# Moving the load of a block's down weights to another queue, and its row numbers one block ahead

## The chip, the core and the metric

The kernel runs on one core of a Trainium2 chip. A core has TensorE (matrix products into PSUM), VectorE, ScalarE and GpSimd for elementwise work, and SyncE, which only issues DMAs. Each engine takes its own instructions in order; they meet by semaphores. DMAs can be issued from the queues of SyncE, ScalarE and GpSimd. The metric is the device time of one execution, in microseconds (us); a value given for a version is the median over runs.

## The reference

One decoder layer on 8 x 128 tokens of width 256: self-attention with a sliding window, cross-attention, and a mixture of 16 experts, top 4, with one shared expert. The part that matters here:

```python
routing_weights = jax.nn.softmax(x @ gate_w.T)             # 1024 tokens, 16 experts
topk_w, topk_ids = jax.lax.top_k(routing_weights, 4)
for e in range(16):
    coef = jnp.sum(jnp.where(topk_ids == e, topk_w, 0.0), axis=-1)
    h = silu_and_mul(x @ w13[e].T)                         # 256 -> 2 x 176 -> 176
    acc = acc + (h @ w2[e].T) * coef[:, None]              # 176 -> 256
out = silu_and_mul(x @ shared_gate_up_w.T) @ shared_down_w.T * sigmoid(x @ sgate_w.T) + acc
```

Everything is float32 with a loose tolerance only for rounding, so the kernel splits most operands of products into a high and a low part and adds three products (helper `three`, L1517).

## The kernel before

It has three stages. Up to about 160 us the attention layers run, tile after tile, with the routing of finished tiles in between. While the first half of the shared expert runs (`rows_of`, `down`), GpSimd scatters each token's normed row to four places in a DRAM table `x_slots` (L538), sorted by expert, and VectorE makes a table of blocks: an expert's rows are padded to whole blocks of 128, and there are always NBLK = 47 blocks. `table` holds for each block its expert and its first row. Then comes the stage of the blocks, and last the second half of the shared expert, the gathering of each token's four results, and the output.

The stage of the blocks is a software pipeline over n = 0 to 46, written out by hand on every engine. For block n:

- SyncE, `load_rows(n)` (L420): reads the first row's number from `table` into a register (L425) and loads 128 rows of 1072 bytes from `x_slots` into `xb` (L426). `xb` has RB = 4 buffers; from block 4 on it waits until TensorE has turned the buffer's previous block (`xbt_psum`) and VectorE has taken its row numbers (`ids_ready`).
- SyncE, `load_down(n)` (L428): reads the expert's number (L432) and loads its down weights, 256 KB, into `w2`, also with 4 buffers (L433); from block 4 on it waits for the down product of the buffer's previous block (`yb_psum`). Three `load_down` are issued as soon as the table is there; then SyncE waits for the scatters and issues `load_rows` 0 to 4, and then per step one `load_rows(n + 5)` and one `load_down(n + 3)`.
- TensorE: `turn_block(n)` (L1772) transposes `xb`; `block_up(n)` (L1524 by way of `three`) multiplies by gate and up weights, which all lie in SBUF; `turn_hidden(n)` (L1792) transposes the hidden rows; `block_down(n)` (L1802) multiplies by `w2`. In iteration n it does `turn_block(n + 2)`, `block_up(n + 1)`, `turn_hidden(n)`, `block_down(n - 1)`. Every fifth iteration it reads a word with six packed expert numbers between `block_up` and `turn_hidden` (L1751).
- ScalarE, in iteration n: `take_rows_t(n + 2)` (L812, the high part `xbt_h`), `block_gate(n + 1)` (L820, `sg`), `take_hidden_t(n)` (L827, `hbt`). Ahead of the loop it does the shared expert's last `high_hidden` (L749, `hid_h`), then `take_rows_t(0)`, `take_rows_t(1)` and `block_gate(0)`.
- VectorE, in iteration n: `low_rows_t(n + 2)` (L1270, `xbt_l`), `block_hidden(n + 1)` (L1278, `hb`), `block_ids(n + 1)` (L1290, L1293, L1294: which output row each row of the block goes to, and its coefficient), `take_block(n - 1)` (L1285, `yb`).
- GpSimd, `place_rows(n)` (L613): scatters `yb` to `y_picks` in DRAM by the numbers `ids`.

Of the kernel before, what the change touches and what calls it, by code (L numbers as in the profile page):

```python
# [17 lines left out]
B, T, D = 8, 128, 256  # L18
# [10 lines left out]
NE, HE, HS = 16, 176, 704  # L29
# [29 lines left out]
def decoder_layer(nc, x_in, ctx_in, keys_in, wqkv_in, bqkv_in, wo_in, bo_in, rope_in, masks_in, gate_in,  # L59
                  w13_in, w2_in, shared_in, ident_in, iota_in, tri_in, upto_in, table_in, picks_in, dump_in, packs_in, out):  # L60
    ctx = ExitStack()
    with ctx:
# [315 lines left out]
        @block.sync  # L378
        def _(sp):
            sp.dma_start(x[:, 0:2, 0:D], x_in[0:2].rearrange("b p d -> p b d")).then_inc(x_first, 16)  # L380
            sp.dma_start(wqkv[:, :, :], wqkv_in.rearrange("(k p) n -> p k n", p=128)).then_inc(wqkv_loaded, 16)
            sp.dma_start(rope[:, :, :], rope_in).then_inc(rope_loaded, 16)
            sp.dma_start(x[:, 2:B, 0:D], x_in[2:B].rearrange("b p d -> p b d")).then_inc(x_rest, 16)
            sp.dma_start(ctx_sb[:, :, :], ctx_in.rearrange("b p d -> p b d")).then_inc(ctx_loaded, 16)
            sp.dma_start(gate[:, :, :], gate_in.rearrange("(k p) n -> p k n", p=128)).then_inc(gate_loaded, 16)
            sp.dma_start(iota[:, :], iota_in.partition_broadcast(128)).then_inc(gate_loaded, 16)
            sp.dma_start(tri[:, :, :].bitcast(U16), tri_in).then_inc(gate_loaded, 16)
            sp.dma_start(upto[:, :], upto_in).then_inc(gate_loaded, 16)
            sp.dma_start(x[:, 0:B, D + TOPK:D + 2 * TOPK], picks_in).then_inc(gate_loaded, 16)
            sp.dma_start(dump[:, :], dump_in).then_inc(gate_loaded, 16)  # L390
            sp.dma_start(sw_raw[:, :], shared_in[0]).then_inc(sw_loaded, 16)

            def load_keys(c):

                if c:
                    sp.wait_ge(scores_psum[CROSS], 4 * c)
                sp.dma_start(ktc[:, :, :, :].rearrange("p u v n -> p (u v n)"), keys_in[c]).then_inc(ktc_loaded, 16)

            load_keys(0)
            for i in range(4):  # L400
                es = slice(4 * i, 4 * i + 4)
                sp.dma_start(w13[:, es, :, :], w13_in[:, es, :, :]).then_inc(w13_loaded, 16)
            sp.wait_ge(zeros_ready, 1)
            for c in range(1, B):
                load_keys(c)
                if 2 <= c <= SC:
                    sp.wait_ge(swl_ready, c - 1)
                    sp.dma_start(sw_raw[:, :], shared_in[c - 1]).then_inc(sw_loaded, 16)
                if c == 1:
                    sp.dma_start(x_slots[EMPTY:EMPTY + 128, :], zero_b[:, :].bitcast(F32)).then_inc(rows_zeroed, 16)  # L410
                for e in range(NZERO * (c - 1), min(NZERO * c, NE)):
                    sp.dma_start(x_slots[REGION * e:REGION * e + REGION, :].rearrange("(p r) d -> p r d", p=128),
                                 zero_b[:, :].bitcast(F32).unsqueeze(1).broadcast_to([128, REGION // 128, XW])
                                 ).then_inc(rows_zeroed, 16)

            sp.wait_ge(swl_ready, SC)
            sp.dma_start(ends[:, :, :, :], table_in).then_inc(table_loaded, 16)
            sp.dma_start(packs[:, :], packs_in).then_inc(table_loaded, 16)

            def load_rows(n):  # L420

                if n >= RB:
                    sp.wait_ge(xbt_psum, n - RB + 1)
                    sp.wait_ge(ids_ready, n - RB + 1)
                row = sp.value_load(table[0:1, NBLK + n:NBLK + n + 1], min_val=0, max_val=EMPTY)  # L425
                sp.dma_start(xb[:, n % RB, :], x_slots[bass.ds(row, 128), :]).then_inc(xb_loaded[n % RB], 16)  # L426

            def load_down(n):  # L428

                if n >= RB:  # L430
                    sp.wait_ge(yb_psum, n - RB + 1)
                e = sp.value_load(table[0:1, n:n + 1], min_val=0, max_val=NE - 1)  # L432
                sp.dma_start(w2[:, n % RB, :, :].rearrange("p k d -> p (k d)"),  # L433
                             w2_in[bass.ds(e, 1)].rearrange("e p k d -> p (e k d)")).then_inc(w2_loaded[n % RB], 16)

            sp.wait_ge(x3_ready, B)
            sp.wait_ge(table_ready, 3)
            for n in range(RB - 1):
                load_down(n)
            sp.wait_ge(scattered, 16 * TOPK * B)  # L440
            for n in range(RB + 1):
                load_rows(n)
            for n in range(NBLK):
                if n + RB + 1 < NBLK:
                    load_rows(n + RB + 1)
                if n + RB - 1 < NBLK:
                    load_down(n + RB - 1)
            for r in range(RB):
                sp.wait_ge(yb_placed[r], 16 * len(range(r, NBLK, RB)))
            for b in range(B):  # L450
                sp.dma_start(yg[:, b, :, :], y_picks[T * TOPK * b:T * TOPK * (b + 1), :].rearrange("(p k) d -> p k d", k=TOPK)
                             ).then_inc(gathered[b], 16)

            for pair in range(HB // 2):
                sp.wait_ge(x_out_ready, pair + 1)
                sp.dma_start(out[2 * pair:2 * pair + 2].rearrange("b p d -> p b d"), x2[:, 2 * pair:2 * pair + 2, :]
                             ).then_inc(y_stored, 16)
            for b in range(HB, B):
                sp.wait_ge(x_out_ready, HB // 2 + b - HB + 1)
                sp.dma_start(out[b], x2[:, b, :]).then_inc(y_stored, 16)  # L460
            sp.wait_ge(y_stored, 16 * (HB // 2 + HB))
# [159 lines left out]
        def _(act):  # L621
# [185 lines left out]
            def take_rows_t(n):  # L807

                act.wait_ge(xbt_psum, n + 1)
                if n >= 2:  # L810
                    act.wait_ge(gu_psum, n - 1)
                act.activation(xbt_h[:, n % 2, :, :], ps_xt[n % 2][:, 0:KC * 128].rearrange("p (k n) -> p k n", k=KC),  # L812
                               ACT.Copy).then_inc(xbt_high, 1)
# [8 lines left out]
            def take_hidden_t(n):  # L822

                act.wait_ge(hbt_psum, n + 1)
                if n >= 2:
                    act.wait_ge(yb_psum, n - 1)
                act.activation(hbt[:, n % 2, :, :], ps_ht[n % 2][:, 0:KC * 128].rearrange("p (k n) -> p k n", k=KC),  # L827
                               ACT.Copy).then_inc(hbt_ready, 1)

            take_rows_t(0)  # L830
            take_rows_t(1)
            block_gate(0)
            for n in range(NBLK):
                if n + 2 < NBLK:
                    take_rows_t(n + 2)
                if n + 1 < NBLK:
                    block_gate(n + 1)
                take_hidden_t(n)
# [8 lines left out]
        def _(dve):  # L847
# [419 lines left out]
            def low_rows_t(n):  # L1267

                dve.wait_ge(xbt_high, n + 1)
                dve.tensor_tensor(xbt_l[:, n % 2, :, :], ps_xt[n % 2][:, 0:KC * 128].rearrange("p (k n) -> p k n", k=KC),  # L1270
                                  xbt_h[:, n % 2, :, :].bitcast(F32), ALU.subtract).then_inc(xbt_low, 1)

            def block_hidden(n):

                dve.wait_ge(sg_ready, n + 1)
                if n >= 2:
                    dve.wait_ge(hbt_psum, n - 1)
                dve.tensor_tensor(hb[:, n % 2, 0:HE], sg[:, n % 2, :], ps_gu[n % 2][:, HE:GU], ALU.mult).then_inc(hb_ready, 1)  # L1278
# [8 lines left out]
            def block_ids(n):  # L1287

                dve.wait_ge(xb_loaded[n % RB], 16 * (n // RB + 1))
                link(dve.scalar_tensor_tensor(found[:, n % 2, :, :], xb[:, n % RB, D:D + TOPK].unsqueeze(1).broadcast_to([128, 2, TOPK]),  # L1290
                                              of_block[:, n:n + 1], xb[:, n % RB, D + TOPK:XW].rearrange("p (i k) -> p i k", i=2),
                                              ALU.is_equal, ALU.mult))
                link(dve.tensor_reduce(offset[:, n % RB, :], found[:, n % 2, :, :], AX.X, ALU.add))  # L1293
                dve.scalar_tensor_tensor(ids[:, n:n + 1], offset[:, n % RB, 0:1], UNPLACED, dump[:, n:n + 1], ALU.add, ALU.min  # L1294
                                         ).then_inc(ids_ready, 1)

            dve.wait_ge(table_ready, 3)
            low_rows_t(0)
            low_rows_t(1)
            block_hidden(0)  # L1300
            block_ids(0)
            for n in range(NBLK):
                if n + 2 < NBLK:
                    low_rows_t(n + 2)
                if n + 1 < NBLK:
                    block_hidden(n + 1)
                if n + 1 < NBLK:
                    block_ids(n + 1)
                if n >= 1:
                    take_block(n - 1)  # L1310
            take_block(NBLK - 1)
# [607 lines left out]
```

## Time and profile before

| What | Value |
|---|---|
| time, median of 3 runs | 344.32 us (343.75 to 344.35) |
| the profiled execution | 343.41 us, of which the span is 341.6 us |
| busy, share of the span: PE / PEld / DVE / ACT / POOL | 90% / 70% / 71% / 55% / 43% |
| mean rate of the DMAs over the span | 196 GB/s |
| DMA queue of SyncE (q1), share of 16 engines | 55.0% |
| DMA queue of ScalarE (q10), share of 16 engines | 1.2% |
| down weights: issues, size, median time to landing | 47, 256.0 KB, 3.1 us |
| rows of a block: issues, size | 47, 134.0 KB |

PE is TensorE's products, PEld its weight loads, which overlap with them; DVE is VectorE, ACT ScalarE, POOL GpSimd. A "q" behind an engine's name marks its queue: register work, waits and the issue of DMAs, which aren't counted as busy. In a timeline the figure in brackets is how long the engine stood idle before the instruction and what ended that. The granted clock is TensorE's, as a share of 2.4 GHz.

### The profile page before, as it was taken

The numbers are of one execution on the slowest core, as the hardware profiler recorded it, in microseconds if no ns is written. First come the engines' busy times: TensorE is split into PE (matmuls) and PEld (weight loads), VectorE is DVE, ScalarE is ACT, GpSimd is POOL, SyncE is SP. The second block draws the span as 40 slices with busy tenths as digits, with TensorE's granted clock in tenths as the row PEclk, the third lists the DMA queues.
The fourth block names the chain that finished last, engine by engine and source line by source line (L and its number), as shares of the span: only waits on it lengthen the run. The fifth ranks groups of instructions, "written<-read, shape, count | busy, mean of one in ns | idle before, by whom it ended". The sixth has DMA issues, their size and how long they took to land.

```text
span 341.6 us, 8504 instructions
## 1 busy us (share of the span) xinstructions
PE 308.8 (90%) x2606; PEld 238.2 (70%) x2608; DVE 241.5 (71%) x720; ACT 186.7 (55%) x538; POOL 146.6 (43%) x179
## 2 busy tenths in 40 slices
PE   6897899999999997879997789998999989999983
PEld 2354576667667764658775578787978979888862
DVE  2357788988888799563887856576766666765396
ACT  1052889888898977473697333343434434342231
POOL 3584133544544413487578253333434434345000
PEclk9999999999999998996999989999999999999998
DMA  7997197989899941023122526777777777774681
GB/s 210 302 389 307 25 310 179 302 248 291 242 264 266 239 141 33 16 98 113 54 94 96 157 66 187 214 218 233 209 230 210 220 224 213 229 220 149 249 319 61
DMA packets 44153, 66.84 MB, mean 196 GB/s; under 512 B 5347, under 2 KB 31988, under 8 KB 43604
## 3 DMA queue, kind: packets, MB, share of 16 engines
q1 hardware_dynamic: 39476, 54.91, 55.0%
q0 software_dynamic: 3792, 10.56, 8.1%
q10 hardware_dynamic: 848, 0.92, 1.2%
q8 instruction: 19, 0.31, 0.4%
q14 instruction: 18, 0.15, 0.2%
HBM read 37.07 MB, written 29.30 MB: 194 GB/s over the span
## 4 chain that ended last, share of the span: by engine, by line
PE 53%; DVE 9%; DMA 8%; issue 8%; SPq 8%; POOL 7%; ACT 6%; DVEq 0%; ACTq 0%; POOLq 0%
PE bank L1524 16%; PE bank L1802 6%; DMA xb<-x_slots 6%; POOL x_slots L538 5%; PE bank L1441 5%; PE bank L1450 5%; ACT probs L650 4%; PE bank L1394 3%; PE bank L1459 3%; SPq L425 3%; PE bank L1772 2%; SPq L432 2%; PE bank L1483 2%; PE bank L1792 2%; PE bank L1562 2%
## 5 line engine op out<-in xcount | busy, mean ns | idle before, releaser
L613 POOL DMA_INDIRECT y_picks<-yb,ids x47 | 45.1, 960 | 70.0 <-DVE yb L1285 69.4
L650 ACT ACTIVATE probs<-bank,neg_max 128x128 f32<-128x128 f32 x256 | 70.7, 399 | 2.7 <-DVE neg_max L903 2.5
L1802 PE MATMUL bank<-w,hbt 128*128 128x256 f32 x188 | 48.3, 380 | 0.0
L903 DVE TENSOR_REDUCE neg_max<-bank 128x4 f32<-128x512 f32 x64 | 42.1, 683 | 5.8 <-PE bank L1441 5.7
L1450 PE MATMUL bank<-ident,probs 128*128 128x128 f32 x256 | 36.9, 281 | 2.6 <-ACT probs L650 2.6
L812 ACT ACTIVATE xbt_h<-bank 128x256 fp32r<-128x256 f32 x47 | 18.0, 384 | 38.5 <-PE bank L1772 38.4
L538 POOL DMA_INDIRECT x_slots<-x,slots x32 | 34.5, 1080 | 9.3 <-issue 8.9
L1450 PEld LDWEIGHTS bank<-ident,probs 128*128 128x128 f32 x256 | 29.1, 143 | 12.4 <-ACT probs L650 10.3
L1802 PEld LDWEIGHTS bank<-w,hbt 128*128 128x128 f32 x188 | 32.1, 190 | 2.5
L1278 DVE TENSOR_TENSOR hb<-sg,bank 128x176 f32<-128x176 f32 x47 | 15.9, 337 | 24.0 <-ACT sg L820 24.0
L820 ACT ACTIVATE sg<-bank 128x176 f32<-128x176 f32 x47 | 14.9, 317 | 30.2 <-PE bank L1524 30.2
L1270 DVE TENSOR_TENSOR xbt_l<-bank,xbt_h 128x256 fp32r<-128x256 f32 x47 | 19.9, 424 | 11.6 <-ACT xbt_h L812 8.6
L1524 PE MATMUL bank<-w_h,xbt_h 128*128 x94 | 27.5, 373 | 0.0
L1772 PE MATMUL bank<-ident,xb 128*128 128x128 f32 x94 | 18.9, 284 | 6.8 <-DMA xb<-x_slots 6.5
L1285 DVE TENSOR_SCALAR yb<-bank,offset 128x256 f32<-128x256 f32 x47 | 22.7, 483 | 2.0 <-PE bank L1802 2.0
L1524 PE MATMUL bank<-w_h,xbt_l 128*128 x94 | 23.4, 331 | 0.0
L1524 PE MATMUL bank<-w_l,xbt_h 128*128 x94 | 23.3, 330 | 0.0
L1772 PEld LDWEIGHTS bank<-ident,xb 128*128 128x128 f32 x94 | 12.0, 143 | 15.2 <-DMA xb<-x_slots 9.2
L509 POOL TENSOR_TENSOR rstd<-ve,expo 128x1 f32<-128x1 f32 x16 | 9.1, 570 | 26.0 <-DVE ve L953 26.0
L485 POOL TENSOR_TENSOR turned<-qkv,rope 128x320 f32<-128x320 f32 x8 | 6.9, 863 | 29.5 <-DVE qkv L884 29.5
L827 ACT ACTIVATE hbt<-bank 128x256 f32<-128x256 f32 x47 | 18.0, 383 | 1.8 <-PE bank L1792 1.8
L1792 PE MATMUL bank<-ident,hb 128*128 128x128 f32 x94 | 18.0, 273 | 0.7 <-issue 0.5
(175 smaller groups left out, 677.6 us busy)
## 6 DMA issues: line engine op xcount, KB each, us to landing
x_slots<-zero_b SPq DMA_DIRECT2D x16, 1072.0 KB, 10.9
w<-w_in_dram SPq DMA_DIRECT2D x47, 256.0 KB, 3.1
xb<-x_slots SPq DMA_DIRECT2D x47, 134.0 KB
w<-w_in_dram SPq DMA_DIRECT2D x4, 1408.0 KB, 12.6
yg<-y_picks SPq DMA_DIRECT2D x8, 512.0 KB, 7.0
sw_raw<-shared_in_dram SPq DMA_DIRECT2D x6, 384.0 KB, 3.4
ktc<-keys_in_dram SPq DMA_DIRECT2D x8, 256.0 KB, 3.2
ctx_sb<-ctx_in_dram SPq DMA_DIRECT2D x1, 1024.0 KB, 12.6
```

Source lines behind the costliest of these rows:

```text
L538: pool.indirect_dma_start(x_slots[:, :], bass.IndirectOffsetOnAxis(slots[:, TOPK * b + k:TOPK * b + k + 1], 0), x[:, b, :], None).then_inc ...
L613: pool.indirect_dma_start(y_picks[:, :], bass.IndirectOffsetOnAxis(ids[:, n:n + 1], 0), yb[:, n % RB, :], None).then_inc(yb_placed[n % RB] ...
L650: ins = act.activation(probs[:, g, j, :], ps_s[kind][g][:, 128 * j:128 * j + 128], ACT.Exp, bias=neg_max[:, kind, g, j:j + 1])
L812: act.activation(xbt_h[:, n % 2, :, :], ps_xt[n % 2][:, 0:KC * 128].rearrange("p (k n) -> p k n", k=KC), ACT.Copy).then_inc(xbt_high, 1)
L903: dve.tensor_reduce(neg_max[:, kind, g, :], ps_s[kind][g].rearrange("p (j n) -> p j n", j=BLK), AX.X, ALU.max, negate=True).then_inc(max_r ...
L1270: dve.tensor_tensor(xbt_l[:, n % 2, :, :], ps_xt[n % 2][:, 0:KC * 128].rearrange("p (k n) -> p k n", k=KC), xbt_h[:, n % 2, :, :].bitcast( ...
L1285: dve.tensor_scalar(yb[:, n % RB, :], ps_yb[n % 2][:, 0:D], offset[:, n % RB, 1:2], None, ALU.mult).then_inc(yb_ready, 1)
L1450: ins = pe.transpose(ps_s[kind][g][:, 128 * j:128 * j + 128], probs[:, g, j, :], ident[:, :])
L1524: ins = pe.matmul(outs, w, m, start=first and i == 0, stop=last and i == len(todo) - 1, skip_group_check=not (first and last))
L1772: ins = pe.transpose(ps_xt[n % 2][:, 128 * k:128 * k + 128], xb[:, n % RB, 128 * k:128 * k + 128], ident[:, :])
L1792: ins = pe.transpose(ps_ht[n % 2][:, 128 * k:128 * k + 128], hb[:, n % 2, 128 * k:128 * k + 128], ident[:, :])
L1802: ins = pe.matmul(ps_yb[n % 2][:, 0:D], hbt[:, n % 2, k, :], w2[:, n % RB, k, :], start=k == 0, stop=k == KC - 1)
```

## The change

The 47 `load_down` move from SyncE's instructions to ScalarE's. Ahead of ScalarE's loop four of them are issued, for blocks 0 to 3, behind two waits for the table and the attention; in its iteration n, from 2 on, `load_down(n + 2)` stands between `take_rows_t(n + 2)` and `block_gate(n + 1)`. SyncE keeps `load_rows` in its old order. On VectorE `block_ids(0)` and `block_ids(1)` stand ahead of `block_hidden(0)`, and iteration n has `block_ids(n + 2)` in place of `block_ids(n + 1)`.

```diff
--- before.py
+++ after.py
@@ -425,26 +425,14 @@
                 row = sp.value_load(table[0:1, NBLK + n:NBLK + n + 1], min_val=0, max_val=EMPTY)
                 sp.dma_start(xb[:, n % RB, :], x_slots[bass.ds(row, 128), :]).then_inc(xb_loaded[n % RB], 16)
 
-            def load_down(n):
-
-                if n >= RB:
-                    sp.wait_ge(yb_psum, n - RB + 1)
-                e = sp.value_load(table[0:1, n:n + 1], min_val=0, max_val=NE - 1)
-                sp.dma_start(w2[:, n % RB, :, :].rearrange("p k d -> p (k d)"),
-                             w2_in[bass.ds(e, 1)].rearrange("e p k d -> p (e k d)")).then_inc(w2_loaded[n % RB], 16)
-
             sp.wait_ge(x3_ready, B)
             sp.wait_ge(table_ready, 3)
-            for n in range(RB - 1):
-                load_down(n)
             sp.wait_ge(scattered, 16 * TOPK * B)
             for n in range(RB + 1):
                 load_rows(n)
             for n in range(NBLK):
                 if n + RB + 1 < NBLK:
                     load_rows(n + RB + 1)
-                if n + RB - 1 < NBLK:
-                    load_down(n + RB - 1)
             for r in range(RB):
                 sp.wait_ge(yb_placed[r], 16 * len(range(r, NBLK, RB)))
             for b in range(B):
@@ -827,12 +815,26 @@
                 act.activation(hbt[:, n % 2, :, :], ps_ht[n % 2][:, 0:KC * 128].rearrange("p (k n) -> p k n", k=KC),
                                ACT.Copy).then_inc(hbt_ready, 1)
 
+            def load_down(n):
+
+                if n >= RB:
+                    act.wait_ge(yb_psum, n - RB + 1)
+                e = act.value_load(table[0:1, n:n + 1], min_val=0, max_val=NE - 1)
+                act.dma_start(w2[:, n % RB, :, :].rearrange("p k d -> p (k d)"),
+                              w2_in[bass.ds(e, 1)].rearrange("e p k d -> p (e k d)")).then_inc(w2_loaded[n % RB], 16)
+
+            act.wait_ge(x3_ready, B)
+            act.wait_ge(table_ready, 3)
+            for n in range(RB):
+                load_down(n)
             take_rows_t(0)
             take_rows_t(1)
             block_gate(0)
             for n in range(NBLK):
                 if n + 2 < NBLK:
                     take_rows_t(n + 2)
+                if n >= 2 and n + RB - 2 < NBLK:
+                    load_down(n + RB - 2)
                 if n + 1 < NBLK:
                     block_gate(n + 1)
                 take_hidden_t(n)
@@ -1297,15 +1299,16 @@
             dve.wait_ge(table_ready, 3)
             low_rows_t(0)
             low_rows_t(1)
+            block_ids(0)
+            block_ids(1)
             block_hidden(0)
-            block_ids(0)
             for n in range(NBLK):
                 if n + 2 < NBLK:
                     low_rows_t(n + 2)
                 if n + 1 < NBLK:
                     block_hidden(n + 1)
-                if n + 1 < NBLK:
-                    block_ids(n + 1)
+                if n + 2 < NBLK:
+                    block_ids(n + 2)
                 if n >= 1:
                     take_block(n - 1)
             take_block(NBLK - 1)
```

## Rows read from the trace of the kernel before

**Rows 1.** groups, 204 to 314 us: busy us, mean ns, idle us, releaser

```profile
L1792 PEld LDWEIGHTS bank<-ident,hb 128*128 128x128 f32 x90 | 12.4, 141 | 2.6 <-issue 1.7
L1772 PEld LDWEIGHTS bank<-ident,xb 128*128 128x128 f32 x86 | 10.9, 141 | 10.9 <-DMA xb<-x_slots 7.8
```

**Rows 2.** timeline of ScalarE: start us, duration us, operation, idle before

```profile
203.03 0.38 ACT L812 ACTIVATE xbt_h<-bank 128x256 fp32r<-128x256 f32 x1
...
205.25 0.38 ACT L812 ACTIVATE xbt_h<-bank 128x256 fp32r<-128x256 f32 x1 [0.70 <-PE bank L1772]
...
207.51 0.38 ACT L812 ACTIVATE xbt_h<-bank 128x256 fp32r<-128x256 f32 x1 [0.70 <-PE bank L1772]
...
307.94 0.38 ACT L812 ACTIVATE xbt_h<-bank 128x256 fp32r<-128x256 f32 x1 [0.70 <-PE bank L1772]
```

**Rows 3.** timeline of SyncE's queue: start, duration of its DMA issues

```profile
213.06 0.34 SPq L433 DMA_DIRECT2D w<-w_in_dram  x1
214.24 0.34 SPq L426 DMA_DIRECT2D xb<-x_slots  x1
215.44 0.34 SPq L433 DMA_DIRECT2D w<-w_in_dram  x1
...
217.72 0.75 SPq L433 DMA_DIRECT2D w<-w_in_dram  x1
```

**Rows 4.** single lines, durations in ns: number reads and a ScalarE DMA

```profile
L425 SPq TENSOR_LOAD <-table x47: 262/268/503, 193.9 to 303.4; - x47
...
L1751 PEldq TENSOR_LOAD <-words x8: 299/308/572, 191.4 to 273.8; - x8
...
L623 ACTq DMA_DIRECT2D bqkv<-bqkv_in_dram x1: 450/450/450, 1.2 to 1.2; - x1
```

**Rows 5.** chain of the work that ended last, 204 to 312 us: start, duration

```profile
231.13 4.30 DMA xb<-x_slots
```

**Rows 6.** TensorE's word read near 225, a product behind it, a weight load

```profile
L1751 PEldq TENSOR_LOAD <-words x1: 301/301/301, 225.0 to 225.0; - x1
...
225.16 0.56 PE L1524 MATMUL bank<-w_h,xbt_h 128*128 x2
...
251.42 0.20 PEld L1792 LDWEIGHTS bank<-ident,hb 128*128 128x128 f32 x2 [0.53 <-issue]
```

**Rows 7.** timeline of all engines, one block's step

```profile
204.83 0.38 PE L1772 MATMUL bank<-ident,xb 128*128 128x128 f32 x2
...
206.21 0.32 ACT L820 ACTIVATE sg<-bank 128x176 f32<-128x176 f32 x1 [0.58 <-PE bank L1524]
...
206.43 0.38 ACT L827 ACTIVATE hbt<-bank 128x256 f32<-128x256 f32 x1
206.56 0.34 DVE L1278 TENSOR_TENSOR hb<-sg,bank 128x176 f32<-128x176 f32 x1 [0.47 <-ACT sg L820]
...
207.26 0.16 DVE L1294 SCALAR_TENSOR_TENSOR ids<-offset,dump 128x1 uint32<-128x1 f32 x1
...
208.28 0.38 PE L1792 MATMUL bank<-ident,hb 128*128 128x128 f32 x2
```

**Rows 8.** timeline of all engines, start of the block stage

```profile
194.87 0.63 ACT L749 ACTIVATE hid_h<-hid 128x512 fp32r<-128x512 f32 x1 [2.38 <-DVE hid L1174]
...
197.19 0.38 ACT L812 ACTIVATE xbt_h<-bank 128x256 fp32r<-128x256 f32 x1 [1.69 <-PE bank L1772]
197.68 0.42 DVE L1270 TENSOR_TENSOR xbt_l<-bank,xbt_h 128x256 fp32r<-128x256 f32 x1 [0.67 <-ACT xbt_h L812]
...
198.49 0.68 PE L1524 MATMUL bank<-w_h,xbt_h 128*128 x2
```

**Rows 9.** busy time by stretch: length, engines (count), granted clock, DMA share, GB/s

```profile
195.00:196.00 1.00, 0.00 (x0) 0.00 (x0) 1.00 (x3) 0.50 (x1) 0.00 (x0) 1.00 0.39 106
199.00:200.00 1.00, 1.00 (x5) 1.00 (x4) 0.42 (x1) 0.15 (x1) 1.00 (x2) 0.50 0.56 129
264.00:276.00 12.00, 11.89 (x73) 10.54 (x72) 8.23 (x31) 5.03 (x15) 4.79 (x5) 1.00 0.78 225
```

## The prediction

> **What bounds the kernel now.** I first asked for the groups of instructions in the stage of the expert blocks (204 to 314 us, nearly a third of the span) and read the column of idle time. TensorE's weight loads stood 7.8 us there for a block's rows, `xb`, to land, and 1.7 us more on nothing that the profile shows [rows 1]. No row shows a wait for `w2`. Then the time of one block: ScalarE takes the turned rows once a block (`xbt_h`). From the take at 203.03 to the one at 307.94 there are 43 steps, 104.91 us, a mean of 2.44; 28 of the 43 last at most 2.33, and the pair in between that is shown is 2.26 apart [rows 2]. I take 2.27 as the step in which TensorE waits for nothing: 43 x 2.27 = 97.6, so 7.3 us are lost in this stage, and that is all that a change of the queues can win in it.
>
> Why are rows late? SyncE issues two loads a block, and its timeline shows a new DMA every 1.18 to 1.20 us, alternately weights and rows [rows 3]. Two loads are 2.38, more than 2.27, without any wait. SyncE's queue, always running, is slower than TensorE; it falls behind until a row load is issued so late that its 4.30 us to land show [rows 5]. A load is mostly not the DMA: reading the number from SBUF takes 0.27, the DMA 0.34, the rest is register work [rows 3, 4].
>
> Four of the long steps have another cause: TensorE's own read of a packed word stood between two products (steps of 2.70, 2.75, 2.68 and 2.56, together 1.6 us over the pace; the row is such a stop, of 0.53) [rows 6]. The other 5.7 us are `xb`.
>
> **The change, part by part.**
>
> *SyncE loses a load per block.* It keeps about 1.20 us of work per step of 2.27. Its queue stops being late: gain up to 5.7 us. The word read also gains some. At 225.0 it ran before the products ahead of it in the program began (225.16), and that step was not long; it stops TensorE where the queue had just been held up [rows 6]. With rows always early, between none and all of the 1.6 us goes; I take half, 0.8. Sum of the gain: 6.5 us, bounds 5.7 and 7.3.
>
> *Row numbers one block further ahead.* The three small VectorE operations of a block (the last one in the row at 207.26) are the same in number. They free `xb` for SyncE. In the block that is shown, rows were turned at 204.83, and VectorE's numbers in that iteration ended at 207.42 [rows 7]. After the change those are the numbers of the block just turned; before, of the one ahead of it. So a buffer is free 2.6 us after its turn, or 3.05 with the 0.45 us that I put on ScalarE below; 0.85 for the register work brings the DMA to 3.9, and the longest landing of 4.30 to 8.2, against four steps, 9.08, until the buffer's next block is due [rows 5, 7]. With the numbers a step later it would be 10.5, so without this part the wait on the numbers would replace SyncE's slowness in the worst landings. At the start two blocks' numbers, not one, come ahead of the first `hb`: 0.6 us more on VectorE (hidden rows are multiplied at 206.56 for 0.34, numbers end at 207.42), beside the first up product, which takes longer. I cost it at nothing; uncovered it would be 0.6 once.
>
> *ScalarE gains a load per block.* No row shows a number read into a register on ScalarE. Nearest from below: SyncE's whole load, 1.20 [rows 3]. From above: TensorE's read is 0.31 instead of 0.27 and ScalarE's own DMA issue at the kernel's start 0.45 instead of 0.34, which makes 1.20 + 0.04 + 0.11 = 1.35 [rows 4]. A gain is excluded, since nothing is taken off ScalarE. I take 1.24, the row nearest in kind for the read and SyncE's DMA for the same transfer. It is queued behind `xbt_h` and ahead of `sg` and `hbt`; its added wait is for a down product that precedes the turn for which `xbt_h` waits, so it is always met. In the shown block `xbt_h` starts at 205.25, so a load that starts with it ends near 206.55 to 206.65, and `sg` goes from 206.21 to about 206.65, `hbt` from 206.43 to 206.87, `hb` from 206.56 to 207.0, ending 207.35 [rows 2, 7]. TensorE needs that `hb` at 208.28. There are 0.9 us of cover, ScalarE is through by 207.25 and its next turn comes at 207.51. Cost on the path: nothing. This stands on the load running beside `xbt_h` (0.38) and not after it, as the word read at 225.0 ran beside TensorE's products. If the cover is gone, each 0.1 us per block is 4.3 us.
>
> *Four loads before the first block, on ScalarE.* Before, SyncE asked for three of them long before. Now they stand in ScalarE's queue behind the `hid_h` of 194.87 and ahead of the first `xbt_h`, which ran at 197.19 [rows 8]. Starting at 194.9, 4 x 1.24 = 4.96, so `xbt_h` at 199.9 instead of 197.19. From its start to the end of the first `xbt_l` it was 0.91 (197.19 to 198.10); the first up product so starts near 200.8 instead of 198.49: loss 2.3 us. Lower bound nothing, if ScalarE's queue can read ahead while `hid_h` waits; upper bound 4 x 1.35 (2.7) and 0.7 for the clock, 3.4. The clock: TensorE did nothing in the us after 195, and the granted clock was 0.50 in the us after 199, so 1.2 of 2.4 GHz [rows 9]. A longer stand has the same low stretch coming, not a second one, so I put nothing for it; 0.7 is one more up product at that level. The next thing late there is nothing: all four rows have landed by then, and `w2` is needed one block later.
>
> At one place a rule speaks against the change. In the stretch 264 to 276 the 16 DMA engines were busy 0.78 of the time at 225 GB/s [rows 9]; all of it is needed at any pace, and at 2.27 instead of the mean of 2.36 of the five steps that lie in that stretch it would be 0.81. The Trainium skill (DMA: Bandwidth & Descriptors, Issuing engines are not separate DMA queues) says that DMAs from any engine share the same 16 DMA engines, and that issuing from several saves only issue time. If transfers were the limit, the sum by that rule would be the loss at the start alone, 346.6, which is the second rival; the rows have issue time as the limit (two loads of 1.19 against 2.27), and where that holds the rule allows the gain.
>
> **The sum.** The profiled execution took 343.41, 341.6 of it the span. Minus 6.5, plus 2.3: 339.2. What follows the blocks starts from their end and moves with it. The median of the three runs is 0.9 above the profiled one, so I forecast 344.32 - 4.2 = 340.1 us, with its own range of 338.9 to 341.7 (gain 5.7 to 7.3, loss 1.9 to 3.1).
>
> **Rivals.**
> 1. *ScalarE becomes the bound (slower).* Place: the block loop. If the load doesn't run beside `xbt_h`, ScalarE's step is 0.38 + 1.24 to 1.35 + 0.32 + 0.38 = 2.32 to 2.43 [rows 2, 7]. From 2.37 on (2.27 + 4.2/43) nothing is won. At 2.43 it is 43 x 0.16 = 6.9 more, 347.0; one DMA issue of SyncE took 0.75 instead of 0.34 [rows 3], and if such collisions between two queues came in each block it would be far more. For: only 0.9 us of cover for a thing never seen on this engine. Against: the word read at 225.0 ran ahead of queued products, and ScalarE has 0.58 and 0.70 us idle in the shown step [rows 2, 7]. Beside it stands a sentence of the Trainium skill (Perfetto Trace Analysis, DMA Instruction — HWDGE): a sequencer locks the descriptor generator for itself, which could make two queues wait for each other; no run here shows it yet.
> 2. *The transfers are the limit.* If rows land later now that weights come on another queue at the same time, half of the 5.7 stays: 340.1 + 2.9 = 343.0; all 6.5 stay, with the start's loss: 346.6. For: 0.81 busy and a landing of up to 4.30 [rows 5, 9]. Against: in the same stage 28 steps ran at the pace, and the lead is 9.08.
> 3. *The start costs nothing*, because ScalarE's queue reads ahead: 344.3 - 6.5 = 337.8. Against: TensorE's word read, too, came only after its queue's waits had been met.
> 4. *It doesn't do what it says*: SyncE would then still be late for the numbers. That is 344 to 346.6.
>
> **How the numbers follow.** Forecast 0.56, ScalarE the bound 0.17, transfers 0.13, the start free 0.11, the last 0.03. The range leaves out most of the first rival and the worst of the second, about 0.18: 337.7 to 345.0. A measurement of this kernel can tell about 0.2% from no change, 0.7 us. Faster: the forecast, the free start, half of the transfers' cases (0.06): 0.73. Slower: most of ScalarE's cases and the worst of the others, 0.18. Within 0.2%: the rest, 0.09.
>
> **What would show it.** In the profile after: TensorE's idle for `xb` in the block stage near zero (right: under 1 us; wrong: over 3); steps between two `xbt_h` at 2.27 throughout (ScalarE as bound: even steps of 2.32 or more, with no idle ahead of `xbt_h`); the first `xbt_h` near 199.9 and the first up product near 200.8; ScalarE's loads at 1.2 to 1.35; `sg` about 0.45 later behind `xbt_h`. The forecast is wrong if TensorE's weight loads wait for `hb` or `hbt`, or if rows still arrive late with SyncE idle.

## The result, and the profile after

The changed kernel took 340.41 us against 343.18 of the kernel before, medians of 20 runs each, taken side by side; the ratio is 0.989, with a 95% interval of 0.986 to 0.992. This ratio is of the fast runs alone (7 of the 20 after lie over 1.5% above that kernel's fastest run and are left out); the two medians, over all runs, give 0.992. The forecast was 340.1. The profiled execution took 339.23 (span 337.4) against 343.41 (span 341.6), 4.2 less.

Where the 4.2 us lie is read from three points: the start of the last `hid_h` ahead of the blocks, the `xbt_h` of block 3 and that of block 46. From `hid_h` to block 46 the profiled execution took 113.07 us before (194.87 to 307.94) [rows 2, 8] and 109.20 after, 3.9 less. What lies ahead of it ended 0.2 earlier, and what follows, 33.7 us, is 0.1 shorter. So in this pair the change acts in this stage alone, in two parts of opposite sign. (How long the work ahead takes varies: in a second profile of the same changed kernel, a0 below, `hid_h` starts at 198.16 instead of 194.68. That is why stages are compared here and not spans.)

The first is the loop. The groups of the block stage after, as in [rows 1]: busy us, mean ns, idle us and releaser.

```profile
L1795 PEld LDWEIGHTS bank<-ident,hb 128*128 128x128 f32 x94 | 13.4, 143 | 1.2 <-issue 0.2
L1775 PEld LDWEIGHTS bank<-ident,xb 128*128 128x128 f32 x88 | 12.4, 142 | 5.4 <-DMA xb<-x_slots 1.3
```

TensorE's wait for rows fell from 7.8 to 1.3 us, and the stop that no row explained, the word read's, from 1.7 to 0.2. The 43 steps took 98.53 (205.35 to 303.88) instead of 104.91; 40 of them last at most 2.33.

The second part is the start. Timeline of all engines after, as in [rows 8]; the figure in brackets is the idle time before an instruction:

```profile
194.68 0.63 ACT L737 ACTIVATE hid_h<-hid 128x512 fp32r<-128x512 f32 x1 [2.39 <-DVE hid L1176]
195.64 3.56 ACTq L823 DMA_DIRECT2D w<-w_in_dram  x4
199.24 0.66 ACT L800 ACTIVATE xbt_h<-bank 128x256 fp32r<-128x256 f32 x2 [3.93 <-issue]
...
200.30 0.95 PE L1527 MATMUL bank<-w_h,xbt_h 128*128 x2 [3.22 <-DVE xbt_l L1272]
```

ScalarE's four loads fill the time from 195.64 to 199.20. From `hid_h` to the first up product it is now 5.62 instead of 3.62 us (194.87 to 198.49), and to the `xbt_h` of block 3, 10.67 instead of 8.16. The missing half us is the clock: the first two up products took 0.95 instead of 0.68 (198.49 in [rows 8]), and the turn of the hidden rows 0.62 instead of 0.40, here after and then before:

```profile
204.41 0.62 PE L1795 MATMUL bank<-ident,hb 128*128 128x128 f32 x2
202.32 0.40 PE L1792 MATMUL bank<-ident,hb 128*128 128x128 f32 x2
```

Busy time by stretch, as in [rows 9] (the granted clock is the third figure from the end):

```profile
200.00:201.00 1.00, 0.70 (x2) 0.71 (x3) 1.00 (x3) 0.00 (x0) 1.00 (x1) 0.50 0.73 209
203.00:204.00 1.00, 1.00 (x5) 1.00 (x4) 0.57 (x2) 0.27 (x1) 0.00 (x0) 0.50 0.23 21
204.00:205.00 1.00, 1.00 (x7) 0.93 (x6) 0.00 (x1) 0.32 (x1) 0.00 (x0) 0.55 0.47 125
```

And two stretches of the kernel before:

```profile
202.00:203.00 1.00, 1.00 (x8) 0.93 (x8) 0.12 (x2) 0.47 (x2) 0.00 (x0) 0.83 0.00 0
203.00:204.00 1.00, 1.00 (x9) 0.98 (x8) 0.93 (x5) 0.47 (x3) 0.00 (x0) 1.00 0.46 117
```

After TensorE's longer stand (3.22 us idle ahead of the product at 200.30) the clock was still at 0.50 (1.2 GHz) in the us after 203; before, it was full by then. A stretch of 1 us at 0.83 or 0.55 is a mix of 0.50 and 1.00 (at 1.00 for 0.66 and for 0.10 of it), so the clock rose at 202.3 before and at 204.9 after. By the same reading of the us after 198 (0.97 before, 0.53 after) it fell at 198.9 and 198.1: it was low for 3.4 us before and for 6.8 after. The start so lost 2.5 us, the loop won 6.4, and 6.4 - 2.5 = 3.9.

One more thing is new. The queue of SyncE, 206 to 300 us (line, what it waited for, us in all, times, longest), and the issues of the two loads with their median time to landing, in us:

```profile
SPq L424 <- DVE ids L1296: 41.3, 40, 1.6
```

```profile
w<-w_in_dram ACTq DMA_DIRECT2D x47, 256.0 KB, 4.3
xb<-x_slots SPq DMA_DIRECT2D x47, 134.0 KB, 4.2
```

SyncE, which before waited 2.5 us for row numbers in four waits, now waits 1 us for those of each block. And weights take 4.3 us to land, from the issue of the DMA to the arrival of its data, which took 3.1.

### The profile page after: what moved, and what is told of

It reads as the page before. It is cut to its first block, busy times and chain, and to the rows that moved or that the text cites. A ratio compares the mean times of both kernels' runs of the same rounds, so it can differ in the third digit from the quotient of the medians.

```text
span 337.4 us, 8509 instructions
## 1 busy us (share of the span) xinstructions
PE 306.1 (91%) x2608; PEld 238.9 (71%) x2608; DVE 238.8 (71%) x720; ACT 186.4 (55%) x538; POOL 146.6 (43%) x179
## 4 chain that ended last, share of the span: by engine, by line
PE 65%; DVE 13%; ACT 10%; DMA 4%; issue 4%; ACTq 2%; POOL 1%; SPq 0%; DVEq 0%; POOLq 0%
PE bank L1527 22%; PE bank L1805 10%; PE bank L1444 5%; PE bank L1453 4%; ACT probs L638 4%; PE bank L1397 3%; DMA xb<-x_slots 3%; PE bank L1775 3%; PE bank L1795 3%; PE bank L1486 2%; PE bank L1462 2%; PE bank L1565 2%; PE bank L1501 2%; PE bank L1439 2%; DVE neg_max L905 1%
## 5 line engine op out<-in xcount | busy, mean ns | idle before, releaser
L1775 PEld LDWEIGHTS bank<-ident,xb 128*128 128x128 f32 x94 | 13.2, 144 | 8.2 <-issue 2.7
```

The lines of the kernel that those rows point to most:

```text
L1775: ins = pe.transpose(ps_xt[n % 2][:, 128 * k:128 * k + 128], xb[:, n % RB, 128 * k:128 * k + 128], ident[:, :])
```

## The experiments

The numbers of all of them together. Ratio: to the kernel before on the same chip, with its interval. Start: from `hid_h` to the first up product. Loop: the 43 steps from block 3 to block 46. Stage: from `hid_h` to the `xbt_h` of block 46. Landing: medians of rows and weights, over those of the 47 loads for which the profile gives a landing (a dash where it gives none; for rows it gives 23 after, 11 in e8 and 47 in e1 again). The last four columns are of the profiled execution, in us.

| kernel | time | ratio | start | loop | stage | landing |
|---|---|---|---|---|---|---|
| before | 343.18 | 1 | 3.62 | 104.91 | 113.07 | - / 3.1 |
| after | 340.41 | 0.989 [0.986, 0.992] | 5.62 | 98.53 | 109.20 | 4.2 / 4.3 |
| a0, after again | 340.75 | 0.991 [0.987, 0.995] | 5.62 | 97.74 | 108.57 | 4.2 / 4.3 |
| e2, queue alone | 351.67 | 1.022 [1.017, 1.028] | 5.62 | 112.18 | 122.74 | 3.7 / 3.6 |
| e3, numbers alone | 340.46 | 0.989 [0.983, 0.995] | 3.43 | 100.97 | 109.11 | 2.7 / 3.1 |
| e1, loads in a gap | 338.96 | 0.985 [0.980, 0.990] | 3.31 | 99.29 | 107.30 | 4.1 / 4.2 |
| e4, SyncE filled again | 343.93 | 1.000 [0.996, 1.005] | 5.62 | 102.63 | 113.30 | 3.8 / - |
| e5, half the weights | 339.48 | 0.989 [0.985, 0.992] | 2.62 | 101.40 | 108.52 | 2.4 / 2.5 |
| e6, one read more | 340.36 | 0.994 [0.991, 0.997] | 5.59 | 98.05 | 108.84 | 2.9 / 3.1 |
| e7, two reads more | 348.85 | 1.017 [1.010, 1.024] | 5.57 | 105.90 | 116.32 | 2.8 / 3.1 |
| e1 again | 338.07 | 0.984 [0.979, 0.988] | 3.39 | 98.24 | 106.24 | 4.3 / 4.4 |
| e8, gap and behind `hbt` | 336.83 | 0.981 [0.976, 0.986] | 2.62 | 96.62 | 105.34 | 3.1 / 3.2 |

The same kernel's stage differs by 0.6 us (after and a0) to 1.1 (e1 twice) from one profiled execution to another; less than that proves nothing.

**The whole change once more**, beside the first experiments.

> The changed kernel again, as the base of the other runs on this chip. In its profile the 43 steps from the take of block 3's rows to that of block 46's took 98.5 us instead of 104.9, and the take of block 3 stood 2.3 us later than before. Theory (late rows were SyncE's issue time, four loads now stand ahead of the first take): the same again, 4 us less than the kernel before, ratio 0.986 to 0.992. Rival (a chance of two traces): the steps come out at 101 us or more, ratio 0.995 or above.

The loop took 97.74 and the stage 108.57: again 7.2 won in the loop and 2.7 lost at the start.

**The queue alone.** The row numbers stay where they were before:

```diff
-            block_ids(0)
-            block_ids(1)
             block_hidden(0)
+            block_ids(0)
...
-                if n + 2 < NBLK:
-                    block_ids(n + 2)
+                if n + 1 < NBLK:
+                    block_ids(n + 1)
```

> The changed kernel without its second part: the down weights stay on ScalarE's queue, the row numbers come where they were before. Theory of the prediction (the numbers free the buffers, and a step later the landing no longer fits into four steps): numbers end 4.9 + 0.45 us after a block's turn, 0.85 for the read, and a landing of 4.2 make 10.4 against 9.08, so the step goes to 2.4 to 2.6, TensorE waits for xb in most steps, and the time is 3 to 12 us above the full change, no better than before. Rival (the queue alone was the cause, the numbers are an addition that does nothing): steps at 2.27 to 2.32, within 1 us of the full change.

2.2% slower than before. SyncE waited 51.2 us for numbers. The chain of the work that ended last, 291 to 300 us, names every link (start, duration):

```profile
286.32 5.54 DMA xb<-x_slots
...
291.91 0.45 PE bank L1774 x2
292.38 0.28 ACT xbt_h L800
...
293.06 0.34 ACTq L823
...
293.50 0.33 ACT sg L808
293.85 0.34 DVE hb L1280
294.19 0.15 DVE found L1292
294.36 0.17 DVE offset L1295
294.56 0.17 DVE ids L1296
...
294.80 0.27 SPq L425
...
295.52 3.76 DMA xb<-x_slots
299.28 0.04 issue
299.32 0.45 PE bank L1774 x2
```

It is a ring. The turn at 291.91 is that of block 36; the numbers at 294.56 are those of block 35, and free the buffer of block 39, which is turned at 299.32. The ring spans three steps, and its time is 3.61 to the issue (291.91 to 295.52) plus the landing. With the median landing of 3.7 a step is (3.6 + 3.7)/3 = 2.43, with the 5.54 of the landing before it in this chain 3.05; the mean step, 2.61, lies between them. With the numbers one step earlier the same ring spans four steps, and even with 5.5 it is (3.6 + 5.5)/4 = 2.28. That is what the second part of the change is worth: without it the first part makes the kernel slower.

**The numbers alone.** The reverse: SyncE keeps both loads, only VectorE's order is that of after.

```diff
-            block_hidden(0)
             block_ids(0)
+            block_ids(1)
+            block_hidden(0)
...
-                if n + 1 < NBLK:
-                    block_ids(n + 1)
+                if n + 2 < NBLK:
+                    block_ids(n + 2)
```

> The kernel before with only its row numbers one block further ahead. Theory (SyncE's queue is the limit by its own instructions, two loads of 1.19 us a block): steps stay at a mean of 2.40 to 2.45, 103 to 105 us for 43, time within 1 us of before. Rival (the wait for the numbers held SyncE up): steps fall to 99 to 101 us, time 3 to 5 us less, which would make the queue's move needless.

This edit of a few lines gives as much as the whole change. In the loop it won 3.9 us, at the start it lost nothing. SyncE waited for numbers no more, and its DMAs come as follows (timeline of its queue):

```profile
207.08 0.34 SPq L426 DMA_DIRECT2D xb<-x_slots  x1
208.19 0.34 SPq L433 DMA_DIRECT2D w<-w_in_dram  x1
209.35 0.34 SPq L426 DMA_DIRECT2D xb<-x_slots  x1
210.46 0.34 SPq L433 DMA_DIRECT2D w<-w_in_dram  x1
211.62 0.34 SPq L426 DMA_DIRECT2D xb<-x_slots  x1
```

Two loads are 1.11 + 1.16 = 2.27 us, exactly TensorE's step. There is no reserve, and single hold-ups of 0.1 to 0.9 us between two issues are never made up: from the row load at 209.35 to that at 301.84 there are 39 steps, a mean of 2.37. Groups, 204 to 314 us:

```profile
L1773 PEld LDWEIGHTS bank<-ident,xb 128*128 128x128 f32 x88 | 11.6, 141 | 8.0 <-DMA xb<-x_slots 4.5
```

TensorE still waits 4.5 us for rows, and the loop is 3.4 over 97.6. This is the part that moving the load can win.

**SyncE filled again.** The changed kernel, with two number reads, unused, behind every row load of SyncE:

```diff
                 sp.dma_start(xb[:, n % RB, :], x_slots[bass.ds(row, 128), :]).then_inc(xb_loaded[n % RB], 16)
+                for _ in range(2):
+                    sp.value_load(table[0:1, n:n + 1], min_val=0, max_val=NE - 1)
```

> The full change with two reads of a number that nobody uses behind each row load on SyncE, 0.57 us each, so that SyncE is again as busy as with two loads (1.13 + 1.14 = 2.27 us a block) while bytes, queues of the transfers and row numbers stay. Theory (SyncE as busy as TensorE's step of 2.27 has no reserve: each hold-up spends lead that never comes back): the 43 steps go from 98 to 101 to 104 us, time 2.5 to 5.5 us above the full change. Rival (what made rows late was the order of the transfers on one queue, not SyncE's instructions): steps at 98 to 99, time within 1 us of the full change.

No wait for numbers is left in SyncE's queue. Its row loads follow each other by 2.25 us at the least and 2.41 in the mean (206 to 300 us), and the loop is 102.63, 4.1 to 4.9 over the change. TensorE waits for rows:

```profile
L1777 PEld LDWEIGHTS bank<-ident,xb 128*128 128x128 f32 x88 | 11.6, 143 | 8.5 <-DMA xb<-x_slots 5.4
```

With weights on another queue and numbers early, SyncE's instructions alone bring the loss back. Its issue time does count.

**Half the weights.** The kernel before with the same instructions, but half the bytes of each weight load (the product uses the first half twice, so the second half of `w2` is left out):

```diff
-                sp.dma_start(w2[:, n % RB, :, :].rearrange("p k d -> p (k d)"), ...
+                sp.dma_start(w2[:, n % RB, 0, :], ...
...
-                    hbt[:, n % 2, k, :], w2[:, n % RB, k, :], ...
+                    hbt[:, n % 2, k, :], w2[:, n % RB, 0, :], ...
```

> The kernel before with half of each block's down weights left out of the load (the second half of the product uses the first half's weights), instructions on SyncE the same. Theory (SyncE's instructions): a row lands a little sooner behind a shorter transfer, 0.3 to 1.5 us once or twice over the whole loop; steps 103 to 104.5 us, time 0.3 to 1.5 us below before. Rival (the 16 DMA engines are the limit, or the landing is): steps at 98 to 100, time 4 us or more below before.

I was wrong here: 3.9 us faster, though SyncE issues as much as ever. Rows landed in 2.4 us, at most 3.2 (of the 12 for which the profile gives it), SyncE waited 0.2 us for numbers instead of 2.5, and the loop was 101.40. In the kernel before, then, bytes are not without a price. I put it down to the ring of [rows 5, 7] (2.59 us from a turn to the end of the next numbers, 207.42 - 204.83, and 0.85 of register work): it takes (3.44 + 4.30)/3 = 2.58 a step with the longest landing and (3.44 + 3.2)/3 = 2.21 with 3.2, so in the longest landings it had no more reserve than SyncE. (Of the 4.6 us that the stage won here 1.0 lie at the start, 3.5 in the loop.)

**Reads on ScalarE.** The changed kernel with one (e6) or two (e7) more unused number reads behind each `load_down` in ScalarE's loop; the edit for one:

```diff
                 if n >= 2 and n + RB - 2 < NBLK:
                     load_down(n + RB - 2)
+                    act.value_load(table[0:1, n:n + 1], min_val=0, max_val=NE - 1)
```

> The full change with one more read of a number per block on ScalarE, behind the load, about 0.66 us. Theory (ScalarE's load lies beside xbt_h and has about 1.0 us of cover ahead of the hb that TensorE needs, and ScalarE's queue is full at about 2.25 a block then): steps between 2.27 and 2.33, 0 to 3 us more. Rival (the load already lies on the path): the step grows by the whole read, 2.9, 27 us more.

> The full change with two more reads per block on ScalarE, 1.3 us. Theory: now ScalarE's queue is the bound, 1.24 for the load, 1.32 for the reads and some 0.35 for handing out three activations, 2.9 a step: 43 x 0.63, 27 us more, with TensorE waiting for hb or hbt. Rival (ScalarE's queue is not the limit even so, or each read counts fully from the first): 0 to 5 us, or 54 us more.

One read costs nothing in the loop (98.05): the cover that the prediction named is there. (The ratio is 0.994 against 0.989 for the change alone, with intervals that overlap.) Two are past its end. Waits of e7, 206 to 300 us:

```profile
ACT sg L808 <- issue: 52.0, 33, 1.8
...
PEld bank L1797 <- DVE hb L1282: 5.8, 16, 0.5
```

Now TensorE waits for `hb`, and steps last 2.46 in the mean, with no idle time ahead of `xbt_h`: the first rival, made real by two reads. Its step is smaller than I expected, so a read costs ScalarE less than I put.

**The loads in a gap.** ScalarE waits 2.4 us ahead of the last `hid_h`. Two loads are put there, behind `gate(SC + 1)`; the others follow in the loop, two blocks ahead instead of four:

```diff
             gate(SC + 1)
+            act.wait_ge(table_ready, 3)
+            for n in range(2):
+                load_down(n)
             high_hidden(SC + 1)
...
-            act.wait_ge(x3_ready, B)
-            act.wait_ge(table_ready, 3)
-            for n in range(RB):
-                load_down(n)
             take_rows_t(0)
...
-                if n >= 2 and n + RB - 2 < NBLK:
-                    load_down(n + RB - 2)
+                if n + 2 < NBLK:
+                    load_down(n + 2)
```

> The changed kernel with only the loads of blocks 0 and 1 ahead of the loop, and those in ScalarE's idle time ahead of the last hid_h (192.3 to 194.7 us in its profile); block n + 2 is loaded in every iteration n from 0. Theory (the start's loss is the four loads in ScalarE's queue): the first up product comes back to 198.3 to 198.9 from 200.3, the steps stay near 98.5, the time is 1.2 to 2.3 us less than with the change alone, 336.9 to 338.0 where that is 339.2. Rival (the first rows or the low granted clock set the start, not ScalarE): the first up product moves by less than 0.5 us and the time with it.

> The version with two weight loads in ScalarE's gap ahead of hid_h, once more, beside the next kernel. Both theories: 338 to 340 us, a ratio of 0.983 to 0.989; rows land 4.0 to 4.2 us after their issue in the median, weights 4.2; 43 steps of 98 to 99.3 us; first up product 3.3 us after the start of hid_h.

Timeline of ScalarE and TensorE in the first of the two:

```profile
194.01 1.46 ACTq L797 DMA_DIRECT2D w<-w_in_dram  x2
196.09 0.63 ACT L737 ACTIVATE hid_h<-hid 128x512 fp32r<-128x512 f32 x1 [2.38 <-DVE hid L1175]
197.56 0.38 ACT L811 ACTIVATE xbt_h<-bank 128x256 fp32r<-128x256 f32 x1 [0.84 <-PE bank L1774]
199.40 0.67 PE L1526 MATMUL bank<-w_h,xbt_h 128*128 x2
```

The wait ahead of `hid_h` is the 2.38 it was; the loads lie in it, and the first up product follows 3.31 us after `hid_h` again. (It stands at 199.40 and not at 198.3 to 198.9, since `hid_h` came 1.4 us later than in the profile after.) The loss at the start was the four loads in ScalarE's queue, and it was avoidable. The low stretch of the clock is back to 3.4 us as well: all six profiles with the four loads ahead of the loop show 6.8 us, the other six 3.4. (In time, e1 is 1.8 us below a0 on the same chip, with intervals that overlap.)

**The load behind `hbt`.** Row loads and weight loads of the changed kernel are issued almost together, and both land late. This kernel is that with the loads in the gap, with the loop's load moved:

```diff
-                if n + 2 < NBLK:
-                    load_down(n + 2)
                 if n + 1 < NBLK:
                     block_gate(n + 1)
                 take_hidden_t(n)
+                if n + 2 < NBLK:
+                    load_down(n + 2)
```

> As the version with the loads in the gap, but in the loop ScalarE's weight load stands behind hbt instead of behind xbt_h, so that it is issued about 1 us away from SyncE's row load. Theory A, rows and weights land late (4.1 and 4.2 instead of 2.7 and 3.1 us) because the two queues issue at the same moment: both medians fall to 3.0 to 3.4, 43 steps of 97.6 to 98.2, 0 to 1.5 us below the version in the gap. Theory B, they land late because of the bytes asked for at this pace, whenever they are issued: medians stay at 4.0 to 4.3, steps and time as in the version in the gap within 0.7 us. Theory C, the load now delays xbt_h (by 0.6 us): TensorE waits for xbt_h, 43 steps of over 100, slower than the version in the gap by 2 us or more.

The issues of a block, first in the changed kernel, then in this one (timeline of the two queues), and this one's issues with their landing:

```profile
227.35 0.37 ACTq L823 DMA_DIRECT2D w<-w_in_dram  x1
227.41 0.34 SPq L426 DMA_DIRECT2D xb<-x_slots  x1
```

```profile
226.06 0.34 ACTq L797 DMA_DIRECT2D w<-w_in_dram  x1
...
227.17 0.34 SPq L426 DMA_DIRECT2D xb<-x_slots  x1
```

```profile
w<-w_in_dram ACTq DMA_DIRECT2D x47, 256.0 KB, 3.2
xb<-x_slots SPq DMA_DIRECT2D x47, 134.0 KB, 3.1
```

Over the 35 row loads between 212 and 292 us, a row load follows the weight load ahead of it by a median of 0.33 us in the changed kernel, 0.24 in e1 again and 1.14 here. Against e1 again, rows land in 3.1 instead of 4.3 us and weights in 3.2 instead of 4.4, at no lower rate of bytes (235 GB/s from 206 to 300, against 232). In e6, where the extra read made it 0.88, they land in 2.9 and 3.1. So it is the moment of issue and not the amount.

Which neighbour matters is not shown, and one run speaks against the row load. In e4 a row load stands 1.30 us behind the weight load ahead of it and 0.97 ahead of the next (medians of the 33 in that stretch), and rows still land in 3.8. A third transfer of each block is GpSimd's scatter of results. By the starts that the profile gives, the weight load nearest to a scatter is a median of 0.14 us from it in the changed kernel, 0.22 in e1 again, 0.16 in e2 and 0.13 in e4, where rows land late, but 0.64 in e6, 0.86 in e3, 1.03 in e7 and 1.00 here, where they land early. So it may be the weights and the scatter that must be kept apart; no run moved the scatter alone.

The loop is the shortest of all, 96.62 (its first step is short, since the `xbt_h` of block 3 was 0.7 late), with no wait of TensorE for rows. At 336.83 this is by its median the fastest kernel of the study, 1.9% below the kernel before; its gain over e1 beside it on the same chip, 1.2 us, lies within the two intervals.

## Why the prediction was right, and where it wasn't

**The sum held.** Predicted: 6.5 won in the loop and 2.3 lost at the start. Measured: 6.4 and 2.5 in the first profile, 7.2 and 2.7 in the second. In time the fall is 2.8 us between the medians (3.7 by the ratio), where 4.2 was forecast. That 340.41 still lies 0.3 from 340.1 is in part luck: the kernel before took 343.18 beside it, and 344.32 in the three runs that the forecast started from. The signs came nearly as described: 1.3 us of waiting for rows (under 1 was asked, over 3 would have been wrong), the first `xbt_h` at 199.24 (199.9) and the first up product at 200.30 (200.8).

**Its account of the loop was half right.** The step "two loads are 2.38, more than 2.27" took its interval where a number read of SyncE was slow (0.36 us at 214.63, instead of 0.27, makes the 1.20 in [rows 3]); unheld, e3 shows 2.27. It is only with hold-ups that SyncE's mean is 2.37. And the prediction gave all of the 5.7 us of `xb` to this one cause. There were two rings without reserve: SyncE's instructions, and the buffer's way from turn to numbers to landing. In the loop 104.91 goes to 100.97 with the numbers alone, and from there to 97.7 to 98.5 with the weights on the other queue: 3.9 for the part that I costed at nothing, 2.4 to 3.2 for the part to which I gave everything. That split holds in this order only: taken first, the moved load costs 7.3 (e2), and the numbers then win 13.7 (112.18 to 98.53). Within the sum, the word read's stops fell by 1.5 (1.7 to 0.2), where 0.8 was taken.

**"The wait on the numbers would replace SyncE's slowness in the worst landings" was too mild.** The prediction had the number and didn't make it a price: 10.5 us for four steps is 2.62 a step and 112.9 for 43, and e2, where SyncE's load is gone and this wait is there, measured 112.18, a mean of 2.61. That the two agree so closely is luck, since the 10.5 has the longest landing in it for every block. It is 7.3 us over before: not in place of SyncE's slowness but twice the loss, 14.6 over 97.6 instead of 7.3. Nor did it see that the same ring, without ScalarE's 0.45, already cost the kernel before 3.9 us (e3), where a wait of 2.5 us in all made it look harmless. This is the step that failed.

**ScalarE's load.** It runs beside `xbt_h`, as supposed, and the four at the start took 1.07 us each (3.56 less one issue of 0.35, over three) instead of 1.24. The number read itself is slower here than on SyncE (0.27 in [rows 4]); duration in ns, least, median and most:

```profile
L822 ACTq TENSOR_LOAD <-table x47: 277/365/706, 194.7 to 303.9; - x47
```

`sg` follows `xbt_h` by 1.12 to 1.79 us (median 1.21) instead of 0.96, so 0.25 later in the median and 0.83 at most where I said 0.45, and e6 and e7 show where the cover ends.

**The start.** Loads of 1.07 make the stand 2.0 us rather than 2.3; the clock, which I put at nothing with 0.7 as the upper bound, cost the other 0.5 to 0.7. "The same low stretch, not a second one" was wrong: it lasted 6.8 us instead of 3.4. The two errors nearly cancel, which is luck. The third rival, that ScalarE's queue reads ahead, fell: its first number read came at 194.7, with `hid_h`.

**The transfers, second rival.** Half of it was true and it didn't matter. Rows do land later, 4.2 instead of 2.7 (e3), though the DMA engines' busy share only rose from 0.74 to 0.81 (206 to 300 us, before and after). With four steps for the ring there is room for that. The Trainium skill (DMA: Bandwidth & Descriptors, Issuing engines are not separate DMA queues) says that issuing from several engines saves only issue time; the runs agree on what it saves (e4), and show that the place of the issue within the step counts too: rows and weights land over a third later in e1 again (4.3 and 4.4) than in e8 (3.1 and 3.2).

**Left open.** What holds SyncE up singly for 0.1 to 0.9 us in e3 (the longest lies in the issue of one row load, 1.25 us at 263.45; number reads took up to 0.50), and what the three long steps of the changed kernel (2.83, 2.38 and 2.62) had in common, no run told apart. Nor did any tell whether the late landings come from the row load or from GpSimd's scatter beside the weight load, nor where such transfers wait for each other.

## What to carry to other kernels

A wait in a pipeline is the sum of a ring: follow it from the buffer's use through every engine back to the next landing, count the steps that it spans, and do so for each part of a change alone; the small reordering was worth as much here as the whole change. When work goes to another queue, look for a gap for it at the start and for its place within the step: moving one load by about 1 us within the step brought its landing from 4.4 to 3.2 us here. A forecast whose total comes true has not shown its parts; the two runs that each made half of the change did.

## What was not expected of the hardware

- Issued 0.33 us apart from two queues, a row load of 134 KB and a weight load of 256 KB land in 4.2 and 4.3 us (after); issued 0.88 to 1.14 apart, in 2.9 to 3.1 and 3.1 to 3.2 (e6, e8). Distance between these two is not all: in e4 rows issued 1.30 us behind the weight load landed in 3.8, and there, as after, GpSimd's scatter started a median of 0.13 and 0.14 us from the weight load.
- Two queues held each other's issue up by no more than 0.05 us, even where the issues overlap (227.35 for 0.37 and 227.41 for 0.34): in the changed kernel the issues of weights took 344 to 388 ns and those of rows 337 to 385, all 47 of each. (Single long issues occur with one queue and with two: one of 1.25 us in e3, one of 1.00 in e6.)
- After TensorE stood 2 us longer, the granted clock was at 0.50 for 6.8 us instead of 3.4, up to 204.9, though TensorE was busy from 201 on.
